# Cross-attention and routed FFN on one core: fp32 projections as three fp32r products, λ in ScalarE's copy, all turns as transposes

## The reference

```python
def _L0_xattn_ref(encoder_feature, decoder_feature, Wq, Wk, Wv, lambda_q1, lambda_q2, lambda_k1, lambda_k2):
    q = decoder_feature @ Wq.T
    k = encoder_feature @ Wk.T
    v = encoder_feature @ Wv.T
    ...
    att = jax.nn.softmax(jnp.einsum('bhtd,bhnd->bhtn', q, k) * scale, axis=-1)
    att = att.reshape(b, HEADS, 2, t, n)
    att = att[:, :, 0] - lam * att[:, :, 1]
    out = jnp.einsum('bhtn,bhnd->bhtd', att, v)
def _moe(x, gate_w, w_gate, w_up, w_down, ws_gate, ws_up, ws_down):
    shared = jax.nn.silu(x @ ws_gate) * (x @ ws_up) @ ws_down
    scores = jax.nn.sigmoid(x.astype(jnp.float32) @ gate_w.T.astype(jnp.float32))
    topk_w, topk_idx = jax.lax.top_k(scores, TOP_K)
    ...
x = x + _L0_xattn_ref(ctx_1024, _layernorm(x, axis=-1), ...)
x = x + _L0_ffn_ref(_layernorm(x, axis=-1), ...)
```

## Time and profile before

| | |
|---|---|
| median of 3 runs | 2420.38 us |
| the profiled execution | 2422.28 us |
| its span, first to last instruction | 2420.5 us |
| mean granted TensorE clock | 0.965 |
| busy: TensorE, VectorE, GpSimd, ScalarE | 90%, 64%, 58%, 56% |
| one step, in steady state | 400 us for 15 steps |

### The profile page before, as it was taken

One profiled execution on the slowest core, in us unless ns is written; L12 is line 12 of the kernel. 1 busy time (PEld: TensorE's weight loads), 2 busy tenths in 40 slices (PEclk: granted clock), 3 DMA queues, 4 the chain that ended last, 5 costly groups with the idle time before them and its releaser, 6 DMA issues.

```text
span 2420.5 us, 76756 instructions
## 1 busy us (share of the span) xinstructions
PE 2184.8 (90%) x20013; PEld 1438.5 (59%) x20014; DVE 1537.4 (64%) x4701; ACT 1352.8 (56%) x3107; POOL 1402.9 (58%) x2249
## 2 busy tenths in 40 slices
PE   5899999999999999999999999999874998989886
PEld 3455555555655565556555555555543766667775
DVE  2567777777777777777777777777633665633333
ACT  1566666666666666666666666666532444434332
POOL 4366666666666666666666666666541554545554
PEclk7899999999999999999999999999966999989999
DMA  5676656655665556555656565656308888867663
GB/s 137 177 224 178 174 162 171 171 168 160 173 172 165 169 163 171 166 170 168 176 160 172 158 175 161 174 164 172 108 28 272 279 272 255 262 186 211 205 204 115
DMA packets 583271, 432.38 MB, mean 179 GB/s; under 512 B 434070, under 2 KB 507930, under 8 KB 582688
## 3 DMA queue, kind: packets, MB, share of 16 engines
q1 hardware_dynamic: 547872, 342.28, 50.9%
q0 software_dynamic: 30720, 84.99, 9.5%
q10 hardware_dynamic: 4608, 4.26, 0.5%
HBM read 235.18 MB, written 200.47 MB: 180 GB/s over the span
## 4 chain that ended last, share of the span: by engine, by line
PE 60%; issue 11%; SPq 11%; DVE 11%; DMA 3%; POOL 2%; ACTq 1%; ACT 1%; DVEq 1%; POOLq 0%; another core or an unknown queue 0%
PE ms_ps L530 10%; PE mx_ps L464 10%; PE o_ps L497 8%; PE mx_ps L696 6%; PE ms_ps L562 5%; PE o_ps L512 3%; DVE mx L870 3%; SPq L320 3%; PE ms_ps L599 3%; PE o_ps L510 3%; PE ms_ps L709 3%; PE o_ps L571 3%; SPq L436 2%; SPq L435 2%; DMA stacks<-mxT 2%
## 5 line engine op out<-in xcount | busy, mean ns | idle before, releaser
L870 DVE TENSOR_REDUCE mx<-mx_ps 128x4 f32<-128x512 f32 x1024 | 703.9, 688 | 424.5 <-PE mx_ps L464 408.2
L752 ACT ACTIVATE prob<-st_ps 128x512 f32<-128x512 f32 x1024 | 612.8, 599 | 574.0 <-PE st_ps L457 561.4
L464 PE MATMUL mx_ps<-stacks 48*128 48x128 bf16 x4096 | 407.2, 221 | 20.3 <-DMA stacks<-mxT 15.9
L457 PE MATMUL st_ps<-stacks 50*128 50x128 bf16 x4096 | 407.4, 220 | 0.5 <-issue 0.5
L464 PEld LDWEIGHTS mx_ps<-stacks 48*128 48x128 bf16 x4096 | 230.1, 95 | 249.9 <-issue 151.7
L497 PE MATMUL o_ps<-prob,v_sb 128*32 128x256 f32 x4096 | 331.8, 396 | 0.2 <-ACT oT L742 0.2
L696 PE MATMUL mx_ps<-w_gu_sb,rows_T 128*128 x1152 | 308.0, 390 | 21.6 <-ACT rows_T L818 19.0
L1071 DVE TENSOR_TENSOR hid<-gate,mx_ps 128x128 f32<-128x128 f32 x288 | 82.9, 288 | 262.0 <-ACT gate L823 220.6
L1264 POOL DMA_INDIRECT rows_dram<-stacks x144 | 141.8, 985 | 171.1 <-DVE stacks L1065 127.0
L457 PEld LDWEIGHTS st_ps<-stacks 50*128 50x128 bf16 x4096 | 230.0, 95 | 5.2 <-issue 3.5
L696 PEld LDWEIGHTS mx_ps<-w_gu_sb,rows_T 128*128 128x128 f32 x1152 | 198.4, 192 | 46.4 <-issue 28.0
(11 more groups left out here) (181 smaller groups left out, 4225.6 us busy)
## 6 DMA issues: line engine op xcount, KB each, us to landing
stacks<-stack_dram SPq DMA_DIRECT2D x512, 192.0 KB
stacks<-rows_dram SPq DMA_DIRECT2D x144, 260.0 KB
stack_dram<-kp SPq DMA_DIRECT2D x128, 256.0 KB, 2.8
stack_dram<-qp SPq DMA_DIRECT2D x64, 384.0 KB
stacks<-rows_dram SPq DMA_DIRECT2D x144, 132.0 KB
stacks<-base_dram SPq DMA_DIRECT2D x144, 128.0 KB
x_in<-in_x SPq DMA_DIRECT2D x64, 256.0 KB, 2.8
c_in<-in_ctxT SPq DMA_DIRECT2D x64, 256.0 KB, 2.9
```

The costliest lines, as they stand in the source:

```text
L457: return pe.matmul(st_ps[k % 2][:, i * P:(i + 1) * P], k_st[p][64 * h:64 * h + KROWS, u, j, :], q_st[p][64 * h:64 * h + KROWS, u, j, :], s ...
L464: return pe.matmul(mx_ps[k % 2][:, i * P:(i + 1) * P], q_st[p][64 * h:64 * h + ROWS, u, j, :], k_st[p][64 * h:64 * h + ROWS, u, j, :], sta ...
L752: nc.scalar.activation(prob[k % 4][:, :], st_ps[k % 2][:, :], ACT.Exp, scale=float(HALF) ** -0.5).then_inc(a_exp, 1)
L870: v.tensor_reduce(mx[:, u, c * CHUNK:(c + 1) * CHUNK], mx_ps[k % 2][:, :].rearrange("p (c n) -> p c n", c=CHUNK), AX.X, ALU.max).then_inc( ...
```

## The change

- Every product on L530, L537, L562 and L571 gets both operands split into a high part rounded to fp32r and a low part (the rest, also as fp32r), and becomes three fp32r matmuls: high by high, high by low, low by high (`product`). Weights are split once at the start: ScalarE writes the high parts, VectorE the low ones, for five tensors.
- Per step the activations are split too: ScalarE's copies of x and of the second norm from PSUM now write `x_hi` and `h_hi` (in place of xnT and h2T), VectorE adds `low` for each (128x512). For the context, ScalarE adds a copy to `c_hi`, GpSimd adds `context_low`; `c_in` has one buffer now, `c_hi` and `c_lo` two each.
- `copy_out` becomes two instructions of 256 columns: a plain copy of the first softmax's half and Identity with the scale `lam_col` (a 128x1 column) for the other. `turn_out` is four transposes; `ident_lam` is gone.
- Slots move. On TensorE: turning x 6 to 0, logits 1 to 0 (now in M0), values 4, 5 to 2, 4, gate and up 0, 2 to 2, 4, counting 6 to 5, q 9, 10 to 8, 9, k 11, 13 to 10, 11. On ScalarE: x_hi in 1, logits' exp 2 to 1, tanh 3 to 5, c_hi in 6, q 11 to 10, second norm 12 to 11, k 14 to 12, h_hi 15 to 14, the norm of x from 4 to 15 of the step before. On GpSimd the norm's chain for x stands after the first scatter.
- On SyncE c_in moves behind x_res and waits for `context_low` (`g_cl`); x_in goes to the end of the step.
- In the expert phase the small buffers lie in `prob` and `v_sb`; its instructions are the same. The written-out steps at the end are two more.

```diff
+            def product(out_ps, still, moving, start, stop):
+                pe.matmul(out_ps, rnd(still[0]), rnd(moving[0]), start=start, stop=False)
+                pe.matmul(out_ps, rnd(still[0]), rnd(moving[1]), start=False, stop=False)
+                return pe.matmul(out_ps, rnd(still[1]), rnd(moving[0]), start=False, stop=stop)
...
                 for gg in range(2):
                     for i in range(2):
                         out_ps, src = TO[:, (2 * gg + i) * P:(2 * gg + i + 1) * P], oT[h % 2][:, gg, i * P:(i + 1) * P]
-                        if i == 0:
-                            mm = pe.transpose(out_ps, src, ident[:, :])
-                        else:
-                            mm = pe.matmul(out_ps, src, ident_lam[:, :], start=True, stop=True)
+                        mm = pe.transpose(out_ps, src, ident[:, :])
...
+                if k == 0 and do_a:
+                    clear(it, "M1", 0)
+                    wait(pe, a_n1, 2, a, 2)
+                    turn(xn, M1, p_xT)
+                if k == 0 and do_r:
+                    clear(it, "M0", 0)
+                    wait(pe, v_hl, 1, r, 1)
+                    logits().then_inc(p_lg, 1)
...
+                if k in (2, 4) and do_b:
                     if k == 2:
+                        clear(it, "M0", 1)
+                    mm = value(b, k // 2 - 1)
...
-                nc.scalar.activation(oT[h % 2][:, :, :].rearrange("p g n -> p (g n)"), o_ps[0][:, :],
-                                     ACT.Copy).then_inc(a_o, 1)
+                nc.scalar.activation(*halves[0], ACT.Copy)
+                nc.scalar.activation(*halves[1], ACT.Identity, scale=lam_col[:, 0:1]).then_inc(a_o, 1)
...
+            def low(s, bank, a_done, high, out, v_done):
+
+                wait(dve, a_done, 1, s, 1)
+                v.tensor_tensor(rnd(out[:, :, :]), bank[:, :], high[:, :, :], ALU.subtract).then_inc(v_done, 1)
...
+            def context_low(s):
+
+                wait(gp, a_ch, 1, s, 1)
+                g.tensor_tensor(rnd(c_lo[s.par()][:, :, :]), c_in[:, :, :], c_hi[s.par()][:, :, :], ALU.subtract).then_inc(g_cl, 1)
...
+                if xs.is_in(1, NS):
+                    wait(sp, g_cl, 1, xs)
+                    sp.dma_start(c_in[:, :, :],
+                                 ctxT[bass.ds(xs.idx(), 1)].rearrange("g p k t -> (g p) k t")).then_inc(d_c, 16)
```

More of the change, by code:

```diff
@@ L139, in program @@
         x_in = sb("x_in", [P, 2, D])
-        c_in = [sb(f"c_in{i}", [P, DK, SW]) for i in range(2)]
+        c_in = sb("c_in", [P, DK, SW])
+        c_hi = [sb(f"c_hi{i}", [P, DK, SW]) for i in range(2)]
+        c_lo = [sb(f"c_lo{i}", [P, DK, SW]) for i in range(2)]
+        w_hi, w_lo = sb("w_hi", [P, 3, DK, D]), sb("w_lo", [P, 3, DK, D])
+        ws_hi, ws_lo = sb("ws_hi", [P, DK, 2 * HID]), sb("ws_lo", [P, DK, 2 * HID])
+        gw_hi, gw_lo = sb("gw_hi", [P, DK, E]), sb("gw_lo", [P, DK, E])
         x_res = [sb(f"x_res{i}", [P, 2, D]) for i in range(2)]
         xn = sb("xn", [P, 2, D])
-        xnT = sb("xnT", [P, DK, SW])
+        x_hi, x_lo = sb("x_hi", [P, DK, SW]), sb("x_lo", [P, DK, SW])
         v_sb = [sb(f"v_sb{i}", [P, VW]) for i in range(2)]
@@ L153, in program @@
         rowt = [sb(f"rowt{i}", [P, 2, RW]) for i in range(2)]
-        h2T = sb("h2T", [P, DK, SW])
+        h_hi, h_lo = sb("h_hi", [P, DK, SW]), sb("h_lo", [P, DK, SW])
         sh_t = sb("sh_t", [P, SW])
@@ L272, in program @@
         RT = 10
-        first, lo, hi, end = -4, 4, NS - 4, NS + 2
+        first, lo, hi, end = -4, 4, NS - 6, NS + 2
         def wait(eng, sem, inc, s, j=0, last=None, plain=False):
@@ L536, in value, with gate_up, logits @@
                 for h in range(DK):
-                    mm = pe.matmul(M0[:, u * SW:(u + 1) * SW], c_in[s.par()][:, h, u * P:(u + 1) * P], w_in[:, 2, h, :],
-                                   start=(h == 0), stop=(h == DK - 1))
+                    mm = product(M0[:, u * SW:(u + 1) * SW], [c[s.par()][:, h, u * P:(u + 1) * P] for c in (c_hi, c_lo)],
+                                 [w[:, 2, h, :] for w in (w_hi, w_lo)], h == 0, h == DK - 1)
+                return mm
+            def gate_up(k):
+                for h in range(DK):
+                    mm = product(M1[:, k * SW:(k + 1) * SW], [w[:, h, k * HID:(k + 1) * HID] for w in (ws_hi, ws_lo)],
+                                 [t[:, h, :] for t in (h_hi, h_lo)], h == 0, h == DK - 1)
+                return mm
+            def logits():
+                for u in range(2):
+                    for h in range(DK):
+                        mm = product(M0[:, u * E:(u + 1) * E], [t[:, h, u * P:(u + 1) * P] for t in (h_hi, h_lo)],
+                                     [w[:, h, :] for w in (gw_hi, gw_lo)], h == 0, h == DK - 1)
                 return mm
@@ L578, in side @@
                     turn_out(d, 3)
[L579 to L589 removed]
+                if k == 5 and do_r:
                     clear(it, "TO", 2)
@@ L605, in side @@
                     turn_out(it, h)
-                if k in (9, 10) and do_a:
+                if k in (8, 9) and do_a:
+                    if k == 8:
+                        clear(it, "M1", 2)
+                        wait(pe, v_x, 1, a, 1)
+                    mm = project(0, (x_hi, x_lo), M1, k - 8)
                     if k == 9:
-                        clear(it, "M1", 2)
-                    mm = project(0, xnT, M1, k - 9)
-                    if k == 10:
                         mm.then_inc(p_q, 1)
@@ L614, in side @@
                     turn_max(b, 0)
-                if k in (11, 13) and do_a:
+                if k in (10, 11) and do_a:
+                    if k == 10:
+                        clear(it, "M0", 3)
+                        wait(pe, g_cl, 1, a, 1)
+                    mm = project(1, (c_hi[a.par()], c_lo[a.par()]), M0, k - 10)
                     if k == 11:
-                        clear(it, "M0", 2)
-                        wait(pe, d_c, 16, a, 16)
-                    mm = project(1, c_in[a.par()], M0, (11, 13).index(k))
-                    if k == 13:
                         mm.then_inc(p_k, 1)
-                if k == 14 and do_d:
+                if k == 13 and do_d:
                     clear(it, "M1", 3)
@@ L778, in step @@
                                              ACT.Copy).then_inc(a_v, 1)
-                    if k == 7 and do_a:
-                        wait(act, p_xT, 1, a, 1)
-                        wait(act, p_q, 1, a)
-                        nc.scalar.activation(xnT[:, :, :], M1[:, :], ACT.Copy).then_inc(a_x, 1)
+                    if k == 6 and do_a:
+                        wait(act, d_c, 16, a, 16)
+                        wait(act, p_v, 1, b, 1)
+                        nc.scalar.activation(rnd(c_hi[a.par()][:, :, :]), c_in[:, :, :], ACT.Copy).then_inc(a_ch, 1)
                     if k == 8 and do_r:
@@ L806, in step @@
                         wait(act, p_su, 1, d)
-                        nc.scalar.activation(h2T[:, :, :], M1[:, :], ACT.Copy).then_inc(a_h, 1)
+                        nc.scalar.activation(rnd(h_hi[:, :, :]), M1[:, :], ACT.Copy).then_inc(a_h, 1)
+                    if k == 15 and do_xs:
+                        wait(act, d_x, 16, xs, 16)
+                        wait(act, p_xT, 1, xs)
+                        norm(xs, x_in, mv1, nb1, xn, g_nb1, a_n1)
             steps(act, step)
```

201 lines of the change are left out of this document (101 added, 100 removed).

## The result

| | before | after |
|---|---|---|
| median (lowest to highest) | 2417.3 us (2400.1 to 2423.5, 4 runs) | 2453.6 us (2441.7 to 2458.1, 4 runs) |
| ratio | | 1.0154, 95% interval 1.0089 to 1.0219 |
| profiled execution; span | 2422.3; 2420.5 | 2456.3; 2454.5 |
| first down projection (slot 7) | 131.61 us | 136.33 us |
| last down projection | 1807.88 us | 1871.27 us |

The prediction was 2365 us, faster. It is wrong in sign, and outside its range of 2300 to 2445. The table says where: the start costs the 4 us foreseen (4.7), the steps lose 59 us where 61 were to be won, and the last part, foreseen as unchanged, is 29 us shorter.

A forecast was written before the change was run, and what follows sets the result against it. TensorE was taken as the bound, by its own work. That work (22.5 us) plus waits (3.2) gave a 25.7 us step; 2422.3 - 61 for the steps + 4 for the start = 2365 us, range 2325 to 2410.

The forecast's parts named there:

- 22.5 + 3.2 = 25.7: The steps: TensorE's own work plus waits gives a step of 25.7 us, 0.96 less than 26.67, 64 times: -61 us.
- TensorE's own work goes from 25.3 to 22.5: TensorE in a step: fp32r groups -1.6 us, logits +0.43, turn_out -0.92, groups that now meet -0.7.
- Rival 1: TensorE's products: fp32r costs two passes or shows its loads, 0.11 us more per matmul, +5.1 a step, 2691 us; 6%.
- `copy_out` 0.75: ScalarE's copy of outputs, split into two halves, one scaled by lambda, would occupy 0.75 us for 0.5 before.
- VectorE 20.9 busy, under 22.5: VectorE in a step: two added subtractions of 0.68 us raise 19.5 us busy to 20.9, below TensorE's 22.5.
- New waits 3.2: TensorE's waits in a step: 3.0 us in three stretches plus 0.2 for an unexplained late exp in slot 14.
- Stretch 1: Slots 12 to 0: TensorE waits 1.5 us for ScalarE, at attend of slot 15 and the turn of x.
- stretch 3: Slot 2: the values wait 0.4 us for M0, which the logits' exp clears, behind exp and x_hi.
- Stretch 2: Slots 5 to 7: attend waits for copy_out and the down projection for v's copy on ScalarE, 1.1 us.
- The clock at 1.2 GHz in parts of the steps: Sign of being wrong: TensorE's clock falls because it idles more; doubted since the expert phase keeps 0.96 at 86% busy.
- Rival 2: Slower: ScalarE's late signals and longer operations make waits of 5.3 us, step 27.8, 2499 us; 14%.
- Rival 3: Maxima come late, since their transfers on SyncE stand behind c_in: 1.1 us a step, 2438 us; 8%.

The follow-up runs named there:

- turns: The kernel before with only lambda moved into ScalarE's copy of outputs (two halves) and all four turns of turn_out as transposes; 2479.1 us, 1.032 of the kernel before.
- c_lo_later: The changed kernel with GpSimd's subtraction for the context's low part behind the maxima instead of ahead of them; 1.044 of the kernel before, mean step 28.12 us.
- three_den: three with four fill transposes each in slots 6 and 7, VectorE's sum of the two best scores moved later and the choice in slot 4; 0.976 of the kernel before.
- after again: The changed kernel, unchanged, run again on one chip with the kernel before; 2454.1 us, 1.014 of the kernel before.
- before again: The kernel before, unchanged, run and traced again on that same chip; 2425.9 us, ratio 1.002.
- three: The changed kernel with logits ahead of x's turn, choice in slot 5, counting in slot 6, and the maxima's transfer between the stacks' halves; 2397.7 us, 0.989 of before.

## Why the prediction was wrong

The step that failed is the one from TensorE's own work to the step: "22.5 + 3.2 = 25.7". It adds to TensorE's work only waits for ScalarE, holds VectorE below TensorE with no waits of its own, and puts the clock at 1.00. Beyond its own work the step has 5.0 us and not 3.2: by the intervals 3.8 of waits and 1.2 in intervals with low clock. Own work adds 0.3 to the miss. Three things are shown: the waits for VectorE are 1.6 us in a step for 0.3, VectorE's operations under GpSimd are stretched, and the low clock costs time in the run with the turns alone. How the 5.0 us divide between VectorE and the clock in the changed kernel stays open, since shortening one stretched operation (c_lo_later, three_den) gave nothing and filling the waits gave 0.0 to 0.4 us. Term by term:

- "TensorE's own work goes from 25.3 to 22.5": right, 22.8. One fp32r pass with its load hidden costs 0.12 (0.11). Rival 1 is out. By the Trainium skill's rule on row groups (TensorE: Matmul & The Clock Gate, "The mechanism") full-height loads would show and make it 0.21, an estimate from 0.10 for the load and 0.11 for the columns; the trace shows 0.12.
- "`copy_out` 0.75": 0.63 in the timeline (442.40 to the next exp at 443.03). The half with lambda has a record of 486 ns, the other 395: by the Trainium skill (ScalarE: Activation LUTs, "What ACT_TABLE_LOAD costs") 93 ns more, and the trace agrees with 91. In the row of operations the plain half takes 0.27 to the next start and the half with lambda 0.36, so the 0.75 had both halves too long.
- "VectorE 20.9 busy, under 22.5": **this failed.** 1004.49 / 43.3 steps = 23.2 us. The two subtractions are priced right. Of the 2.3 us more, den, hots and hotp are 1.6, and four others of the same kind (mxp, hot and rowt twice) 0.5. I counted durations from the old order and took them over into a new one, where they overlap otherwise. VectorE's own busy time is longer than TensorE's own work.
- "New waits 3.2": 3.8, and partly at other places. Stretch 1 has 1.2 for 1.5 (0.96 at the turn, 0.2 in slot 15), stretch 3 0.32 for 0.4. Stretch 2 has 1.3 for 1.1, but for VectorE's sh_h and maxima and hardly for v. Not foreseen: slot 5 (0.74), since I looked at the operands of the counting and not at who holds its bank; the prediction had its wait vanish.
- "The clock at 1.2 GHz in parts of the steps": named as what would show it wrong, and held off with the expert phase, which is 86% busy at 0.96. **That argument failed too**: turns is busier than that phase (1101 us of 1200, 92%) and falls to 0.93; filled, at 95%, it is at 1.00.
- Rival 2 (slower, 2499) had the sign; but the waits for ScalarE are no longer than forecast, and what was added stands at VectorE and in the clock. The late signal itself, 1.29 us in slot 14, is halved in the changed kernel (0.68 on average). Rival 3's wait for mxT is real but smaller than its 1.1: 19.1 / 43.3 = 0.44 us a step, 0.2 in after again.
- "The expert phase: 0": -29 us. Before, TensorE waits there for ScalarE's copies, after the change not. The waits of before (2160 to 2400 us), then of after (2220 to 2434 us):

```profile
PE mx_ps L696 <- ACT rows_T L818: 18.8, 23, 1.9
```

```profile
PE mx_ps L722 <- ACT prob L853: 2.3, 1, 2.3
```

ScalarE of the kernel before stands still there with its input ready: the products for `gate` (first row) are done at 2290.81, and between its copy at 2290.70 and `gate` at 2292.94 it does nothing.

```profile
2289.72 1.09 PE L696 MATMUL mx_ps<-w_gu_sb,rows_T 128*128 x4
...
2290.70 0.38 ACT L818 ACTIVATE rows_T<-st_ps 128x256 f32<-128x256 f32 x1 [1.28 <-PE st_ps L688]
...
2292.94 0.28 ACT L823 ACTIVATE gate<-mx_ps 128x128 f32<-128x128 f32 x1 [1.86 <-PE mx_ps L696]
```

What makes it stand was not tried. It is no merit of the change's arithmetic: on one chip this part took 599 us in the changed kernel (after again), 614 in the kernel before (before again), and 614 in three, whose instructions there are the changed kernel's.

Sum: 4.7 + 59 - 29 = +34 us, the difference of the two profiled executions.
